# The experts' down product in split operands over 128 rows, and TensorE's expert numbers four at a time

## The reference, cut to what matters

```python
logits = x2 @ gate_w.T                       # 16 experts, each row goes to its 4 best
top_w, top_i = jax.lax.top_k(softmax(logits), 4)
gu = einsum('th,eih->tei', x2, w1)           # I = 176: 176 gate and 176 up columns of an expert
act = silu(gu[..., :176]) * gu[..., 176:]
down = einsum('tei,ehi->teh', act, w2)       # 176 -> 256
routed = einsum('te,teh->th', wfull, down)
shared = silu(sg) * su @ sh_down_w.T         # an expert of 352 columns for all rows
return hid + routed + shared
```

## Time and profile before

| | |
|---|---|
| median of 3 runs | 1223.82 us (1223.71 to 1224.97) |
| the profiled execution's own time | 1221.95 us |
| its span, first to last instruction | 1220.2 us |
| mean granted TensorE clock | 0.990 |
| busy PE / DVE / ACT / POOL | 1160.6 / 846.3 / 799.6 / 580.7 us |
| the chain that ended last, by engine | PE 76%, DVE 8%, ACT 6%, issue 4%, POOL 3%, DMA 2% |

### The profile page before, as it was taken

One profiled execution on the slowest core, in us unless ns is written; L12 is line 12 of the kernel. 1 busy time (PEld: TensorE's weight loads), 2 busy tenths in 40 slices (PEclk: granted clock), 3 DMA queues, 4 the chain that ended last, 5 costly groups with the idle time before them and its releaser, 6 DMA issues.

```text
span 1220.2 us, 25017 instructions
## 1 busy us (share of the span) xinstructions
PE 1160.6 (95%) x7868; PEld 988.4 (81%) x7868; DVE 846.3 (69%) x2663; ACT 799.6 (66%) x2069; POOL 580.7 (48%) x844
## 2 busy tenths in 40 slices
PE   6999999899999999999999999999998879999986
PEld 5766566689999989999989999889986769999962
DVE  5778888576677667876677876668865755555535
ACT  3587888677778776778776787777786524444422
POOL 4063655454334444457343466334453446666650
PEclk9999999999999999999999999999999989999998
DMA  8965555256631211213121131211114237777766
GB/s 271 284 190 168 173 175 170 89 176 191 189 114 57 91 51 57 81 53 123 35 69 37 35 109 67 69 36 54 64 54 132 78 112 116 118 119 118 119 110 223
DMA packets 111779, 139.58 MB, mean 114 GB/s; under 512 B 11364, under 2 KB 94820, under 8 KB 111524
## 3 DMA queue, kind: packets, MB, share of 16 engines
q1 hardware_dynamic: 97204, 119.10, 32.2%
q0 software_dynamic: 14448, 18.88, 9.5%
HBM read 63.36 MB, written 61.87 MB: 103 GB/s over the span
## 4 chain that ended last, share of the span: by engine, by line
PE 76%; DVE 8%; ACT 6%; issue 4%; POOL 3%; DMA 2%; SPq 1%; POOLq 0%; ACTq 0%; DVEq 0%
PE bank L1500 56%; PE bank L1742 5%; PE bank L1926 5%; PE bank L1561 2%; DVE bank L1127 2%; PE bank L1597 2%; PE bank L1614 2%; POOL xs_rows L684 1%; PE bank L1604 1%; PE bank L1905 1%; PE bank L1936 1%; ACT pT L842 1%; POOL sum_rows L746 1%; ACT p L966 1%; DVE hs L1358 1%
## 5 line engine op out<-in xcount | busy, mean ns | idle before, releaser
L1127 DVE CUSTOM_DVE_ANT_0 bank<-bank,mask 128x512 f32<-128x512 f32 (+3 forms) x512 | 235.1, 522 | 42.3 <-PE bank L1500 21.6
L957 ACT ACTIVATE p<-bank,stat 128x512 f32<-128x512 f32 (+3 forms) x256 | 131.6, 527 | 127.0 <-DVE stat L1127 127.0
L537 POOL CAST w_hl<-raw_qkv 128x512 fp32r<-128x512 f32 x96 | 58.8, 613 | 301.9 <-DMA raw_qkv<-in_qkvo 154.2
L1500 PE MATMUL bank<-xT,w_hl 128*128 128x512 f32 x768 | 190.3, 396 | 0.0
L1500 PEld LDWEIGHTS bank<-xT,w_hl 128*128 128x128 f32 x768 | 142.2, 188 | 37.1 <-issue 2.0
L746 POOL DMA_INDIRECT sum_rows<-mid,goal x79 | 122.9, 1555 | 70.7 <-DVE mid L1464 68.1
L966 ACT ACTIVATE p<-p,stat 128x512 f32<-128x512 f32 (+3 forms) x256 | 123.1, 553 | 14.7 <-DVE stat L1361 14.7
L538 POOL TENSOR_TENSOR w_hl<-raw_qkv,w_hl 128x512 fp32r<-128x512 f32 x96 | 124.2, 1294 | 7.8
L1383 DVE TENSOR_TENSOR o<-bank,o 128x512 fp32r<-128x512 f32 x64 | 44.2, 690 | 109.4 <-ACT o L973 109.4
L1500 PE MATMUL bank<-pT,v 128*128 128x256 f32 (+2 forms) x576 | 117.1, 348 | 0.0
L1500 PE MATMUL bank<-k,q 128*128 128x512 f32 (+2 forms) x576 | 111.5, 337 | 2.5 <-ACT pT L950 1.7
(11 more groups left out here) (248 smaller groups left out, 2561.3 us busy)
## 6 DMA issues: line engine op xcount, KB each, us to landing
raw_qkv<-in_qkvo SPq DMA_DIRECT2D x32, 768.0 KB, 5.3
xs_rows<-blank SPq DMA_DIRECT2D x32, 520.0 KB, 3.3
xs_rows<-blank SPq DMA_DIRECT2D x5, 2730.0 KB, 14.6
xrow<-xs_rows SPq DMA_DIRECT2D x79, 130.0 KB, 2.5
raw_o<-in_qkvo SPq DMA_DIRECT2D x32, 256.0 KB, 3.6
sum_rows<-blank SPq DMA_DIRECT2D x3, 2176.0 KB, 8.5
stk<-xT SPq DMA_DIRECT2D x96, 64.0 KB
stk<-k_hl SPq DMA_DIRECT2D x96, 64.0 KB
```

The source lines that it names most:

```text
L537: link(pool.tensor_copy(hi, raw))
L957: act.activation(p2[:, n % 2, POFF[qi]:POFF[qi + 1]], s2(t), ACT.Exp, scale=-1.0, bias=stat2[:, 0, n % 2, t:t + 1], accum_out=stat2[:, 1, ...
L1127: return dve.tensor_tensor_reduce(scores, scores, mask[:, TB - scores.shape[1]:], scale=-1.0, scalar=-2.0 * MASKED, op0=ALU.add, op1=ALU.m ...
L1500: ins = pe.matmul(out, a, b, start=start and i == 0, stop=stop and i == len(pairs) - 1, **kw)
```

## The change

1. **Down product.** The 176 inner rows are no longer 88 + 88. The first 128 (block A) are multiplied in split operands: ht_hi with w2a HI, ht_lo with w2a HI, ht_hi with w2a LO. The other 48 (block B) are put twice into one block of 128 rows, hx columns 128 to 175 and 192 to 239, the rest of it zero; the weight w2b has the rounded weights in partitions 0 to 63 and the rests in 64 to 127, so that two matmuls (ht_hi and ht_lo with w2b) do all of B. That is 5 float32r matmuls of 256 columns.
2. **Around it.** DVE writes the product into hx in two instructions (128 columns, and 2 x 48). ACT writes ht_hi, DVE then ht_lo. The scaled result moves from DVE to ACT, and stands there before ht_hi. DVE keeps goal, with a semaphore e_goal of its own, for which POOL and SP wait as well.
3. **Weights.** w2a is fetched raw in 8, 7, 8 and 7 pieces where w2r was, w2b in 12, 10, 12 and 10 pieces after the last of them, ahead of row tile 4. They are converted in place: ACT rounds A (`round_a`, s = 4, 9, 10 and iteration 0), POOL makes its rest (`rest_a(0)` after `shared_lo(4)`, the others after the sends), POOL rounds B's upper half (`round_b`; two before the scatters, two at scatters 2 and 4), ACT and DVE make its lower half (`copy_b`, `rest_b`: before iteration 0 and at 1, 4, 7).
4. **PE.** Expert numbers come four at a time, without the bounds check, between down and turn_h. The waits in turn_tile, up and turn_h for what a later wait implies are gone.

The diff, cut to its core:

```diff
@@ SP
+                for e, src, first, m in pieces_a(q):
+                    sp.dma_start(w2a_raw[first:first + m, e, 1, :], src).then_inc(w2a_in[q], 16)
...
             for i in range(NX // 2):
                 load_tile(i)
             load_w2(B - 1)
+            sp.wait_ge(f_dn, SHARED)
+            for q in range(B):
+                for e, src, first, m in pieces_b(q):
+                    sp.dma_start(w2b_raw[first:first + m, e, :], src).then_inc(part_in[q], 16)
             for i in range(NX // 2, NT):
                 load_tile(i)
@@ POOL
+            def rest_a(q):
+                own = block_of(q)
+                pool.wait_ge(w2a_round, q + 1)
+                pool.tensor_tensor(w2a[:, own, 1, :], w2a_raw[:, own, 1, :], f32(w2a[:, own, 0, :]), ALU.subtract)\
+                    .then_inc(w2_pool, 1)
             for s in range(1, LO_POOL):
                 shared_lo(s)
+                if s == 4:
+                    rest_a(0)
             for j in range(TPB):
                 send_tile(B - 1, j)
+            rest_a(1)
+            round_b(0)
+            rest_a(2)
+            round_b(1)
+            rest_a(3)
             for i in range(NT):
+                if i in (2, 4):
+                    round_b(i // 2 + 1)
+                pool.wait_ge(e_goal, i + 1)
                 pool.wait_ge(e_y, i + 1)
@@ ACT, the loop
+                if i >= 2:
+                    m = i - 2
+                    act.wait_ge(e_dn, m + 1)
...
+                    act.activation(yt[:, m % NY, :], bank[6 + m % 2][:, 0:D], ACT.Copy,
+                                   scale=xt[:, m % NX, D + 1:D + 2]).then_inc(e_y, 1)
+                if 1 <= i <= NT:
                     act.wait_ge(e_ht, i)
+                    act.activation(ht_hi[:, (i - 1) % 2, :], bank[4 + (i - 1) % 2][:, 0:2 * P], ACT.Copy)\
+                       .then_inc(e_htc, 1)
@@ DVE, the loop, after the two products and goal
+                    dve.wait_ge(e_htc, i)
+                    dve.tensor_tensor(ht_lo[:, (i - 1) % 2, :], bank[4 + (i - 1) % 2][:, 0:2 * P],
+                                      f32(ht_hi[:, (i - 1) % 2, :]), ALU.subtract).then_inc(e_htl, 1)
@@ PE, down
-                pe.wait_ge(e_htc, i + 1)
+                    pe.wait_ge(w2_pool, W2_POOL[i // (E // B)])
+                    pe.wait_ge(w2b_rest, i // (E // B) + 1)
+                pe.wait_ge(e_htl, i + 1)
...
+                        [(ht_hi[:, i % 2, first], a_hi), (ht_lo[:, i % 2, first], a_hi), (ht_hi[:, i % 2, first], a_lo),
+                         (ht_hi[:, i % 2, last], w2b[:, ds(expert[i], 1), :].rearrange("p a n -> p (a n)")),
+                         (ht_lo[:, i % 2, last], w2b[:, ds(expert[i], 1), :].rearrange("p a n -> p (a n)"))])\
@@ PE, the loop
-                if i + 1 < NT:
-                    expert.append(pe.value_load(tab[0:1, P + i + 1:P + i + 2], min_val=0, max_val=E - 1))
+                if i % FEW == 0 and i + 1 < NT:
+                    expert += experts_of(slice(P + i + 1, P + min(i + 1 + FEW, NT)))
```

More of the change, by code:

```diff
@@ L84, in sandwich_kernel @@
         hs = sb(ctx, "hs", [P, T, D])
+        with ExitStack() as late_raw:
+            w2a_raw = sb(late_raw, "w2a_raw", [P, E, 2, D])
         with ExitStack() as late:
-            w2r = sb(late, "w2r", [H2E, E, 2, D])
+            w2a = sb(late, "w2a", [P, E, 2, D], F32R)
         xT = sb(ctx, "xT", [P, B, 2, C, TB], F32R)
@@ L350, in routed_pieces, with down_pieces, pieces_a, pieces_b @@
                     k += m
[L352 to L361, removed]
+        def down_pieces(first, count):
+            done = 0
+            while done < count:
+                k, p = (first + done) // P, (first + done) % P
+                m = min(P - p, count - done)
+                yield moe_d[k // MGC, p:p + m, k % MGC, 2 * C * P:], done, m
+                done += m
+        def pieces_a(q):
+            return [(e, *piece) for e in range(E // B * q, E // B * (q + 1))
+                    for piece in down_pieces(SHI + e * EI, EA)]
+        def pieces_b(q):
+            return [(e, src, half * P // 2 + first, m) for e in range(E // B * q, E // B * (q + 1))
+                    for half in range(2) for src, first, m in down_pieces(SHI + e * EI + EA, P // 2)]
+        def block_of(q):
+            return slice(E // B * q, E // B * (q + 1))
         @block.sync
@@ L448, in load_tile @@
                     sp.wait_ge(e_y, i - NX + 1)
-                sp.dma_start(xt[:, i % NX, :], xs_d[ds(row, P), :]).then_inc(e_x[i % NX], 16)
+                    sp.wait_ge(e_goal, i - NX + 1)
+                sp.dma_start(xt[:, i % NX, :], xs_d[ds(row, P), :]).then_inc(rows_in[i % NX], 16)
             for q in range(B - 1):
@@ L997, in w1_half, with round_a, copy_b @@
                    .then_inc(w_hi, 1)
+            def round_a(q):
+                own = block_of(q)
+                act.wait_ge(w2a_in[q], 16 * len(pieces_a(q)))
+                act.activation(w2a[:, own, 0, :], w2a_raw[:, own, 1, :], ACT.Copy).then_inc(w2a_round, 1)
+            def copy_b(q):
+                act.wait_ge(part_in[q], 16 * (1 + len(pieces_b(q))))
+                if q:
+                    act.wait_ge(w2b_rest, q)
+                act.activation(w2b_hi[P // 2:, :, :], w2b_raw[P // 2:, block_of(q), :], ACT.Copy).then_inc(w2b_copy, 1)
             for s in range(SHARED):
@@ L1022, in take_x @@
                 act.wait_ge(e_t, i + 1)
[L1023 to L1025 removed]
+                if i < 2:
                     act.wait_ge(f_dn, SHARED)
@@ L1897, in _, with experts_of @@
             pe.wait_ge(r_tabi, 1)
-            expert = [pe.value_load(tab[0:1, P:P + 1], min_val=0, max_val=E - 1)]
+            FEW = 4
+            def experts_of(tiles):
+                _, values = nc.values_load_multi_w_load_instructions(
+                    tab[0:1, tiles], [mybir.EngineType.PE], min_val=0, max_val=E - 1,
+                    skip_runtime_bounds_check_because="the table's second half counts the experts whose last row lies "
+                                                      "before a tile, and is clamped to E - 1")
+                return list(values)
+            expert = experts_of(slice(P, P + 1))
             def turn_tile(i):
-                pe.wait_ge(e_x[i % NX], 16 * (i // NX + 1))
-                if i >= 2:
-                    pe.wait_ge(e_xl, i - 1)
+                pe.wait_ge(rows_in[i % NX], 16 * (i // NX + 1))
                 for c in range(C):
```

102 lines of the change are left out of this document (59 added, 43 removed).

## The result

| | before | after |
|---|---|---|
| median | 1223.76 us (1222.50 to 1224.97, 4 runs) | 1258.13 us (1255.82 to 1262.82, 4 runs) |
| ratio, 95% interval | | 1.0286 [1.0254, 1.0317] |
| profiled execution, its span | 1221.95, 1220.2 us | 1262.82, 1261.1 us |
| mean granted clock | 0.990 | 0.977 |
| busy PE / DVE / ACT / POOL | 1160.6 / 846.3 / 799.6 / 580.7 us | 1166.6 / 858.6 / 838.6 / 595.4 us |

34.4 us slower; 12.9 had been forecast. The direction and the largest cause were right, but the time lies above the range. I go through the same stages as before.

The account below looks back on a forecast made before the run. PE's iteration of 2.27 us and SP's queue ahead of tile 4 were taken as the bounds. 18.0 + 2.4 + 2.0 + 1.5 + 0.4 - 11.4 = +12.9 us gave a median of 1236.7 us, range 1223 to 1249.

Parts of the forecast that it names:

- ranking and sends, to tile 0's load: Ahead of the loop: rest_a(0) on POOL holds up DVE's ranking, delaying sends and loads by 2.4 us (0 to 2.6).
- SP's queue: Before row tile 4: 51 weight pieces at 0.445 us instead of 12 delay its load by 18.0 us (15.2 to 19.6).
- the expert numbers: PE's loop: four numbers loaded at once cost 0, between a gain of 0.4 and a loss of 4 us.
- clock, conversions, end: Half clock after tile 4's wait +2.0 us, conversions inside the loop +1.5, last two tiles +0.4.
- the iteration: Steady loop, 76 iterations: from 2.27 to 2.12 us each, a gain of 11.4 us (8.4 to 20.5).
- queued work of 1.0 us hides most of it: PE's loop: 5 matmuls and 4 transposes queued behind down hide most of four number loads, up to 4 x 0.30 us.
- the rival of the longer loop: PE's loop: number loads or address work add to 2.16, giving 2.27 us or more, no gain, 1248.1 us; chance 0.14.
- What would show it wrong: Signs: tile 4 before 1012; iteration 2.00 without idle or below 1.95; ranking not lengthened; issue idle every fourth iteration.
- The upper bound of 2.16: Steady loop: chain from down through ACT's two instructions, DVE's ht_lo and PE's address work and weight load closes at 2.16 us.
- the fewer waits are worth nothing: PE's loop: PE is never idle there, so removing three waits, the checks and three loads of four gives 0.
- The rival on the other side: PE's instruction stream bounds the loop; the iteration could fall to 1.86 us, gaining 31.2, total 1216.9 us; chance 0.08.
- The rival of the loop at 2.00: Steady loop runs at PE's own 2.00 us, gaining 20.5 instead of 11.4 us, total 1227.6 us; chance 0.16.

Follow-up runs that it names:

- e0: The changed kernel run again without any edit, as the measure for the other runs: 1256.42 us, ratio 1.0289 to the kernel before.
- e6: The changed kernel with the load of four expert numbers ahead of down instead of behind it: 1247.01 us, ratio 1.0224 to the kernel before.
- e1: The changed kernel with expert numbers loaded one per iteration and checked, ahead of up: 1247.76 us, ratio 1.0222 to the kernel before.
- e5: The kernel before with only PE's new instruction stream (four unchecked numbers at once, three waits gone): 1221.60 us, ratio 1.0009.
- e3: The changed kernel with ACT's scaled result behind ht_hi instead of ahead of it: 1254.54 us, ratio 1.0279 to the kernel before.
- e7: The changed kernel with the edits of e6 and e3 together: 1242.98 us, ratio 1.0188 to the kernel before.
- e10: e9 with POOL's conversions given to DVE and ACT, some loads and ACT's rounding moved: 1214.64 us, ratio 0.9939 to the kernel before.
- e2: The changed kernel with block B's weights laid out by the host, 4 DMAs in place of 44 pieces: 1245.50 us, ratio 1.0205.
- e9: The changed kernel with host-laid weights, one number under ht_lo's wait, ACT and DVE reordered, POOL's conversions moved and spread: 1223.04 us, ratio 1.0010.

## Why the prediction was wrong

Steps against e0's trace and the kernel before, in us of the span:

| step | forecast | measured |
|---|---|---|
| ranking and sends, to tile 0's load | +2.4 (0 to 2.6) | +2.7 (992.10 - 989.42) |
| SP's queue | +18.0 (15.2 to 19.6) | +22.7 (tile 0 to tile 4: 32.26 instead of 9.54) |
| tile 4 to the end | -7.5 | +11.7 |
| of it the expert numbers | 0 (-0.4 to +4) | +9.9 (e0 less e6, tile 4 to the end) |
| of it clock, conversions, end | +3.9 | about +4.1 (a remainder: e6's 223.0, less 221.2, and 76 x 0.03 = 2.3 gained) |
| of it the iteration | -11.4 (-20.5 to -8.4) | -2.3 |
| sum | +12.9 | +37.1 |

So of the 24.2 us between forecast and trace, 9.9 are the expert numbers, 9.1 the iteration, 4.7 SP's queue, and 0.5 all else.

*The step that failed most* is "queued work of 1.0 us hides most of it". That work is queued only if the sequencer is past the load while PE still has work. But PE's sequencer stood at down's wait for ht_lo until 1104.63; when it was let go, only down's 0.60 us were ahead of the load, and the 1.00 us stuck out: turn_h came 0.64 later than behind an ordinary down (1.33 less 0.69). Part of that PE would have waited before the next down in any case, so the iteration took 2.76 instead of 2.24, and 19 times 0.52 is 9.9. The prediction names this very thing, in the rival of the longer loop ("PE's sequencer is held at down's wait, so it no longer runs ahead"), and then argues against it with the 1.0 us of queued work, which includes what stands behind the load. Even its bound of 0.2 x 19 = 4 was too low: e1 and e6 gain 8.7 and 9.4 us by the medians (8.2 and 7.9 by the ratios), and 10.1 and 9.9 from tile 4 to the end in the traces, and e5 shows that the same load costs nothing where the wait ends early. What would show it wrong, idle time put down to issue in every fourth iteration, is what the trace had.

*The iteration, 2.24 instead of 2.12.* The chain was the right one, and its terms hold, but for one: S to ACT's start 0.89 (0.80 and the exposed weight load's 0.10), ht_hi's record 0.38, hand-over 0.03, ht_lo 0.42, hand-over to down 0.15 (0.14 was forecast). ACT's scaled result, however, holds its engine 103.80 - 103.43 = 0.37 and not 0.28: I had its length from a copy without a scale. That makes 2.24, and taking 2.12, a value below the chain, cost the rest. The upper bound of 2.16 was none. e3 and e7 confirm the place: with ACT's order turned round the iteration is 2.10.

*SP's queue.* The count and the place were right, the price too low: (1024.36 - 995.91) / 51 = 0.56 each, where 0.445 was taken. The 0.39 of the last group of before was not the price of a piece here, 0.47; why the same kind of issue is dearer here, no run shows. The range's high end mixed the right 0.61 for 64 rows with that 0.39.

*Right* were: the direction; the ranking held by rest_a(0), at its length; a wait of 10.06 us for tile 4, and half clock after it (what it costs was not measured by itself); down at 0.12 a matmul; that the fewer waits are worth nothing (e5). The rival on the other side, PE's instruction stream as the bound, is refuted by e5: 1.0009 [0.9995, 1.0022]. The rival of the loop at 2.00 was nearer to the truth than it looked: reordered, the loop reaches 2.10, which is its 2.00 and the first weight load of down, still exposed (0.21 from the first to the second matmul of down in e10's rows, where 0.12 is the step without it), since down still waits for ht_lo until 0.15 before it starts.

*What e2 adds* is that the terms don't add up: SP's 22.8 us were on the path, and only 10.9 came back with them, since the conversions had hidden below. The prediction had seen them there, but too short: in e0 down(0) starts at 1014.83 and not at about 1006, because ACT had to wait for the first group's pieces until 1007.16, and rest_b(0) took 3.37 beside POOL where it takes 1.22 alone.

## What to carry to other kernels

Before a load or any slow step of a sequencer is counted as hidden, ask what is queued at that moment: behind a wait that ends last, nothing is, and the step belongs ahead of the wait. A queue ahead of the loop is worth what the next thing below it leaves, so look what lies under the wait before it is taken away. And conversions given to an idle POOL are not free for DVE: count them as DVE's time, at POOL's length; here DVE and ACT did them themselves for less (from e9 to e10, 8.4 us, moved loads and a moved wait included).

## What was not expected of the hardware

- Loading numbers on PE's sequencer is charged nearly by the number: four take 1.00 us, one 0.30, so that four at once save only 0.2 of 1.2 us; in e3 four took 1.26 at the median, up to 1.38.
- ACT's copy of 256 columns with a scale for each row holds ACT for 0.37 us, without one for 0.28 (0.27 for ht_hi, 104.07 - 103.80, in the changed kernel).
- A DVE instruction of 1.22 us can be held for 6.64 us by POOL instructions that follow each other, and one of 0.15 us for 2.82.
- A DMA issue on SP costs 0.47 us from start to start for most pieces and 0.63 in a run of 64-row pieces here, and 0.46 for a whole group of 128 rows x 4 x 256 numbers in e10 (0.91 for two): the number of issues counts far more than the bytes.
